# Attention stage: merged score banks, a later reciprocal, all normalising on GpSimd, q and k transposed through the projection banks, context scales a head later

## What is computed

```python
xq, wq = quant_dequant(layernorm(x)), quant_dequant(ctx)   # fp8, blocks 1x128 and 128x128
x = x + einsum('emk,enk->emn', xq, wq)
hidden = layernorm(x)                          # second layer starts here
h = rmsnorm(hidden, attn_norm_w)
q, k, v = h @ q_w.T, h @ k_w.T, h @ v_w.T      # 16 q heads, 4 kv heads of 128
q, k = rope(rmsnorm(q)), rope(rmsnorm(k))
p = softmax(causal(q k^T / sqrt(128)))
hidden = hidden + (p v) @ o_w.T
h2 = rmsnorm(hidden, ffn_norm_w)
out = x + hidden + moe(h2)                     # 8 experts, top 2, width 352
```

## Time and profile before

| | us |
|---|---|
| median of 3 runs | 1465.03 |
| lowest and highest | 1464.09, 1466.55 |
| span of the profiled execution | 1464.1 |
| PE busy over the span | 1268.7 (87%) |
| DVE, ACT, POOL busy | 838.2, 719.6, 383.0 |
| prologue | 0 to 91 |
| the 16 iterations | 91 to 1090 |
| dispatch and experts | 1100 to 1464 |

### The profile page before, as it was taken

The page is one execution under the profiler, slowest core; times in us unless marked ns, Lnnn a source line. Parts: engine busy times, 40 slices in busy tenths (PEclk is TensorE's granted clock), DMA queues, the critical chain, the costliest instruction groups (busy, mean ns, idle before and its releaser), DMA issues. The chain is left out here.

```text
span 1464.1 us, 22579 instructions
## 1 busy us (share of the span) xinstructions
PE 1268.7 (87%) x6845; PEld 1022.3 (70%) x6845; DVE 838.2 (57%) x2459; ACT 719.6 (49%) x2289; POOL 383.0 (26%) x545
## 2 busy tenths in 40 slices
PE   1867899999999989889999999989885299999995
PEld 0455676787776778677767778778664288888995
DVE  7667877666876657578757656565535022222321
ACT  6447755556675555466645655546542022222331
POOL 0223221332322223133213133223210123334332
PEclk9889999999999999999999999999997599999998
DMA  3270324350535465547535565764214786774443
GB/s 94 79 266 22 135 109 178 135 200 9 219 101 201 150 217 177 195 140 207 176 130 196 178 215 179 200 201 148 87 58 174 244 293 189 214 234 75 83 76 43
DMA packets 89444, 227.85 MB, mean 156 GB/s; under 512 B 12080, under 2 KB 49840, under 8 KB 79088
## 3 DMA queue, kind: packets, MB, share of 16 engines
q1 hardware_dynamic: 75552, 201.21, 39.2%
q0 software_dynamic: 10848, 24.71, 9.1%
q10 hardware_dynamic: 2928, 0.49, 0.2%
...
## 5 line engine op out<-in xcount | busy, mean ns | idle before, releaser
L527 POOL TENSOR_TENSOR prob<-prob,rtotal 128x128 f32<-128x128 f32 (+2 forms) x192 | 116.9, 614 | 459.1 <-DVE rtotal L1270 439.7
L1264 DVE TENSOR_SCALAR_CACHE_REDUCE prob<-bank,nscale 128x128 f32<-128x128 f32 (+3 forms) x256 | 135.0, 545 | 166.7 <-PE bank L705 166.3
L944 ACT ACTIVATE prob<-prob,bias 128x128 f32<-128x128 f32 (+3 forms) x256 | 144.8, 566 | 154.3 <-DVE prob L1264 153.5
L669 PE MATMUL bank<-w_hi,hT_hi 128*128 128x512 f32 x480 | 175.1, 365 | 15.0 <-DVE rot L1229 14.9
L724 PE MATMUL bank<-pT,v 128*128 128x512 f32 (+3 forms) x512 | 175.0, 444 | 9.7 <-ACT pT L950 9.1
L950 ACT ACTIVATE pT<-bank 128x512 f32<-128x512 f32 (+3 forms) x256 | 103.8, 433 | 140.6 <-PE bank L713 140.0
L1657 PE MATMUL gu<-we,xT_hi 128*128 x624 | 155.8, 332 | 17.0 <-SPq L1599 14.3
L669 PE MATMUL bank<-w_hi,hT_lo 128*128 128x512 f32 x480 | 163.7, 341 | 0.0
L669 PE MATMUL bank<-w_lo,hT_hi 128*128 128x512 f32 x480 | 163.6, 341 | 0.0
L504 POOL TENSOR_TENSOR r<-r,rot 128x640 f32<-128x640 f32 x60 | 99.9, 1666 | 189.8 <-DVE rot L1229 189.8
L1657 PEld LDWEIGHTS gu<-we,xT_hi 128*128 128x128 f32 x624 | 109.0, 190 | 23.4 <-issue 21.4
(11 more groups left out here) (291 smaller groups left out, 2854.5 us busy)
## 6 DMA issues: line engine op xcount, KB each, us to landing
...
```

Of the source, the lines that this page charges most:

```text
L527: nc.gpsimd.tensor_tensor(p, p, rtotal[:, 4 * h + q:4 * h + q + 1].broadcast_to([P, KEYS[q]]), ALU.mult).then_inc(prob_ready, 1)
L669: last = nc.tensor.matmul(o, hT[a][:, k, t * P:(t + 1) * P], wkv(j, c, k) if kv else wq(j, c, k), start=(k == 0 and n == 0), stop=(k == KC ...
L944: nc.scalar.activation(p, p, ACT.Exp, bias=bias[:, 4 * h + q:4 * h + q + 1], scale=-1.0, accum_out=total[:, 4 * h + q:4 * h + q + 1]).then ...
L1264: nc.vector.tensor_scalar(prob[(G * it + h) % (LAG + 1)][:, P_AT[q]:P_AT[q] + KEYS[q]], bank[SC + q % 2][:, 0:KEYS[q]], nscale[it % 2][:, ...
```

## The change

Scores go in three parts: q = 0 and 1 share one bank, q = 2 and q = 3 have one each, in turns over banks 3 and 4; q = 2 is scored before `fill(h, 1)` and q = 3 before `fill(h, 2)`. One reciprocal takes all four sums of a head, one head later, and POOL normalises all four blocks. The transposed probabilities are copied in three copies rather than four (j = 2 and 3 together). ACT takes exponentials 2 before `fill(h, 1)` and exponentials 3 before `fill(h, 2)`, but copies 0 and 1 behind `fill(h, 1)` and copy 2 behind `fill(h, 2)`. q and k are transposed in the order 1, 0, 2, 3, 4 into banks 0 and 1: 1 in `fill(3, 2)`, 0 and 2 in `fill(3, 3)`, 3 and 4 in `fill(0, 1)` of the next iteration, and the projection into these banks waits for all five. The context's maxima are taken in four parts over `fill(0, 1)` and `fill(0, 2)`, POOL's part (`ca`) stands in `fill(0, 3)`, the scales in `fill(1, 1)`. Left out below: semaphore lists, the prologue's and the tail's calls, the same functions' calls with new arguments.

```diff
@@ -98,7 +98,7 @@
-FILL = {(0, 1): (('u', 4),),
+FILL = {(0, 1): (('u', 3), ('u', 4)),
@@ -108,15 +108,16 @@
-        (3, 2): (('o', 3),),
-        (3, 3): (('t', 0), ('t', 1), ('t', 2), ('t', 3))}
-FRONT = ({(0, 1): (('cm', 0), ('cs', 0)),
-          (0, 2): (('cv', 0), ('cr', 0)),
-          (0, 3): (('cv', 1), ('cd', 0)),
-          (1, 2): (('cr', 1),),
-          (1, 3): (('cv', 2),),
+        (3, 2): (('o', 3), ('t', 1)),
+        (3, 3): (('t', 0), ('t', 2))}
+FRONT = ({(0, 1): (('cm', 0), ('cm', 1)),
+          (0, 2): (('cm', 2), ('cm', 3)),
+          (0, 3): (('ca', 0),),
+          (1, 1): (('cs', 0), ('cv', 0)),
+          (1, 2): (('cr', 0), ('cv', 1)),
+          (1, 3): (('cd', 0), ('cr', 1), ('cv', 2)),
@@ -174,6 +175,8 @@
+PARTS = ((0, 1), (2,), (3,))
+TURNS = (1, 0, 2, 3, 4)
@@ -274,7 +277,8 @@
-TR = (PT, PT + 1, AUX, PT, AUX)
+SC_AT = (0, KEYS[0], 0, 0)
+PT_COLS = (QS[0], QS[1], QS[2] + QS[3])
...
@@ -329,6 +333,19 @@
+def score_bank(s, part):
+    return bank[SC + (3 * s + part) % 2]
+def score_reads(fill):
+    return 4 * (fill // 3) + (2, 3, 4)[fill % 3] if fill >= 0 else 0
+def pt_bank(s, m):
+    return bank[PT + (3 * s + m) % 2]
+def turn_bank(i):
+    return bank[TURNS.index(i) % 2]
@@ -521,10 +538,11 @@
-    def normalise(it, h, q):
-        pool.wait_ge(inverted, 16 * it + 4 * h + q + 1)
-        p = prob[(G * it + h) % (LAG + 1)][:, P_AT[q]:P_AT[q] + KEYS[q]]
-        nc.gpsimd.tensor_tensor(p, p, rtotal[:, 4 * h + q:4 * h + q + 1].broadcast_to([P, KEYS[q]]), ALU.mult).then_inc(prob_ready, 1)
+    def normalise(s):
+        pool.wait_ge(inverted, s + 1)
+        for q in range(TT):
+            p, n = prob[s % (LAG + 1)][:, P_AT[q]:P_AT[q] + KEYS[q]], 4 * (s % G) + q
+            nc.gpsimd.tensor_tensor(p, p, rtotal[:, n:n + 1].broadcast_to([P, KEYS[q]]), ALU.mult).then_inc(prob_ready, 1)
@@ -552,27 +570,26 @@
-        work = {"kv": lambda t: add_rope(it + 1, t), "n": lambda _: newton(it + 1), "cm": lambda _: column_maxima(b + 1)}
+        work = {"kv": lambda t: add_rope(it + 1, t), "n": lambda _: newton(it + 1), "ca": lambda _: column_maxima(b + 1)}
         if g == 1 and b:
             add_hidden(b - 1)
         for h in range(G):
-            normalise(it, h, 0)
-            normalise(it, h, 1)
-            for kind, i in units(it, h, 1):
-                if kind in work:
-                    work[kind](i)
-            normalise(it, h, 2)
-            for place in (2, 3):
+            if it or h:
+                normalise(G * it + h - 1)
+            for place in (1, 2, 3):
                 for kind, i in units(it, h, place):
                     if kind in work:
                         work[kind](i)
+    normalise(G * NIT - 1)
 @block.tensor
 def _(pe):
     def transposes_x(f, t, after=None):
         n = TT * f + t
         pe.wait_ge(xd_ready, n + 1)
-        if f and t in (0, 3):
-            pe.wait_ge(qk_lo, (G + 1) * (HKV * (f - 1) + (2 if t == 0 else 3)))
+        if f and t == 0:
+            pe.wait_ge(hlo_ready, TT * f)
+            need(pe, lg_ready, TT * (f - 2))
@@ -617,7 +634,7 @@
-            pe.wait_ge(qk_lo, (G + 1) * min(HKV * (rb + 2), NIT))
+            pe.wait_ge(hlo_ready, TT * min(rb + 3, B))
@@ -661,6 +678,7 @@
+            need(pe, qk_lo, (G + 1) * j)
@@ -671,47 +689,43 @@
-        it = j - 1
-        if i == 1 and j == 0:
-            pe.wait_ge(first_added, TT)
+        turn = TURNS.index(i)
+        if turn == 0:
+            pe.wait_ge(rope_added if j else first_added, TT * (j + 1))
+            need(pe, o_added, TT * (j - 2) + 3 if j >= 2 else 0)
         if i == 0:
             pe.wait_ge(k_ready, j + 1)
-            need(pe, pt_copied, 16 * it + 4 * (G - LAG))
-        if i == 2 and j:
-            b, g = divmod(it, HKV)
-            if g == 1 and b + 1 < B:
-                pe.wait_ge(x1_ready, TT * (b + 1) + 3)
-            if g == 2 and b + 1 < B:
-                pe.wait_ge(hlo_ready, TT * (b + 2))
-            if g == HKV - 1 and b:
-                pe.wait_ge(lg_ready, TT * b)
-        if i >= 2:
-            need(pe, qk_lo, (G + 1) * j + {2: 0, 3: 1, 4: 3}[i])
+            need(pe, o_added, TT * (j - 1) if j >= 2 else 0)
+        if turn >= 2:
+            pe.wait_ge(qk_lo, (G + 1) * j + turn - 1)
         at = G * HD if i == 0 else (i - 1) * HD
         for t in range(TT):
-            last = nc.tensor.transpose(bank[TR[i]][:, t * P:(t + 1) * P], r[:, t, at:at + HD], ident[:, :])
+            last = nc.tensor.transpose(turn_bank(i)[:, t * P:(t + 1) * P], r[:, t, at:at + HD], ident[:, :])
         last.then_inc(qk_tr, 1)
-    def score(it, h, q):
-        if q == 0:
+    def score(it, h, part):
+        s = G * it + h
+        if part == 0:
             pe.wait_ge(qk_lo, (G + 1) * it + h + 2)
-        need(pe, biased, 16 * it + 4 * h + q - 1)
-        o = bank[SC + q % 2]
-        for n, (a, c) in enumerate(SPLITS):
-            nc.tensor.matmul(o[:, 0:KEYS[q]], qT[a][:, h, q * P:(q + 1) * P], kT[it % 2][c][:, 0:KEYS[q]], start=(n == 0), stop=False)
-        nc.tensor.matmul(o[:, q * P:(q + 1) * P], identb[:, :], mask[:, :], start=False, stop=True).then_inc(scored, 1)
-    def transpose_p(s, j):
-        if j == 0:
-            pe.wait_ge(prob_ready, 3 * s + 3)
-            pe.wait_ge(prob3_ready, s + 1)
-        need(pe, pt_copied, 4 * s + j - 1)
-        for q in range(j, TT):
-            last = nc.tensor.transpose(bank[PT + j % 2][:, (q - j) * P:(q - j + 1) * P],
-                                       prob[s % (LAG + 1)][:, P_AT[q] + j * P:P_AT[q] + (j + 1) * P], ident[:, :])
+        need(pe, biased, score_reads(3 * s + part - 2))
+        for q in PARTS[part]:
+            o = score_bank(s, part)[:, SC_AT[q]:SC_AT[q] + KEYS[q]]
+            for n, (a, c) in enumerate(SPLITS):
+                nc.tensor.matmul(o, qT[a][:, h, q * P:(q + 1) * P], kT[it % 2][c][:, 0:KEYS[q]], start=(n == 0), stop=False)
+            last = nc.tensor.matmul(o[:, q * P:(q + 1) * P], identb[:, :], mask[:, :], start=False, stop=True)
+        last.then_inc(scored, 1)
+    def transpose_p(s, m):
+        if m == 0:
+            pe.wait_ge(prob_ready, TT * (s + 1))
+        need(pe, pt_copied, 3 * s + m - 1)
+        at = 0
+        for j in ((0,), (1,), (2, 3))[m]:
+            for q in range(j, TT):
+                last = nc.tensor.transpose(pt_bank(s, m)[:, at:at + P], prob[s % (LAG + 1)][:, P_AT[q] + j * P:P_AT[q] + (j + 1) * P], ident[:, :])
+                at += P
@@ -720,7 +734,7 @@
-        pe.wait_ge(pt_copied, 4 * s + j + 1)
+        pe.wait_ge(pt_copied, 3 * s + min(j, 2) + 1)
...
@@ -772,9 +786,6 @@
-            if h == 0 or s == 0:
-                pe.wait_ge(qk_lo, (G + 1) * it + G)
@@ -783,19 +794,16 @@
-                values(s, 1)
-                transpose_p(s, 3)
-            score(it, h, 3)
-            if s >= 0:
-                values(s, 2)
-                values(s, 3)
+                for j in range(1, TT):
+                    values(s, j)
             fill(h, 3)
     for s in range(G * NIT - LAG, G * NIT):
-        for j in range(TT):
-            transpose_p(s, j)
-            if j:
-                values(s, j - 1)
-        values(s, TT - 1)
+        transpose_p(s, 0)
+        transpose_p(s, 1)
+        values(s, 0)
+        transpose_p(s, 2)
+        for j in range(1, TT):
+            values(s, j)
@@ -944,10 +952,10 @@
-    def copy_p(s, j):
-        act.wait_ge(pt_tr, 4 * s + j + 1)
-        need(act, pv_step, 4 * s + j - 3)
-        nc.scalar.activation(pT[:, PT_AT[j]:PT_AT[j] + QS[j]], bank[PT + j % 2][:, 0:QS[j]], ACT.Copy).then_inc(pt_copied, 1)
+    def copy_p(s, m):
+        act.wait_ge(pt_tr, 3 * s + m + 1)
+        need(act, pv_step, TT * (s - 1) + (1, 2, 4)[m] if s else 0)
+        nc.scalar.activation(pT[:, PT_AT[m]:PT_AT[m] + PT_COLS[m]], pt_bank(s, m)[:, 0:PT_COLS[m]], ACT.Copy).then_inc(pt_copied, 1)
@@ -958,9 +966,9 @@
-        act.wait_ge(qk_tr, (G + 1) * j + i + 1)
+        act.wait_ge(qk_tr, (G + 1) * j + TURNS.index(i) + 1)
         o = kT[j % 2][0][:, :] if i == 0 else qT[0][:, i - 1, :]
-        nc.scalar.activation(o, bank[TR[i]][:, :], ACT.Copy).then_inc(qk_hi, 1)
+        nc.scalar.activation(o, turn_bank(i)[:, :], ACT.Copy).then_inc(qk_hi, 1)
...
@@ -1020,22 +1028,20 @@
+            exponentials(it, h, 2)
+            fill(h, 1)
             if s >= 0:
                 copy_p(s, 0)
                 copy_p(s, 1)
-            fill(h, 1)
-            exponentials(it, h, 2)
+            exponentials(it, h, 3)
+            fill(h, 2)
             if s >= 0:
                 copy_p(s, 2)
-                copy_p(s, 3)
-            fill(h, 2)
-            exponentials(it, h, 3)
-            if s >= 0:
                 hi_attn(s)
             fill(h, 3)
     for s in range(G * NIT - LAG, G * NIT):
-        for j in range(TT):
-            copy_p(s, j)
+        for m in range(3):
+            copy_p(s, m)
...
@@ -1108,12 +1114,6 @@
-    def ctx_maxima(f):
-        for k in range(KC):
```

(48 more changed lines are left out.)

## The result

The changed kernel takes **1555.49 us** (median of 4 runs, 1552.87 to 1557.49) against 1465.1 of the kernel before on the same chip: 1.062 times as long, 95% interval 1.059 to 1.065. The forecast was 1458, with 1482 as its upper end. The profiled execution has a span of 1554.6 us.

What follows compares the result with a forecast made beforehand. PE was taken as the bound, with its idle 86.1 us and low clock to win. Terms 19 + 12 + 13 + 2 - 17 - 20 - 2 = 7 us off 1464.1, plus 0.9, gave 1458 us; range 1437 to 1482.

Steps and rivals of the forecast that it cites:

- (d): Copy 2 behind ACT's fill 2 delays values 2: loss of 20 us, bounds 5 and 30; copies 0 and 1 covered.
- R2: Rival: ACT's copy behind the fills decides, its waits and the first projection's bringing half clock: 1480 us, chance 0.28.
- R1: Rival: the waits really go, ACT and DVE being lighter than taken: 1441 us, chance 0.20.
- (a): Iteration ends, PE waiting for k's low half: 1.1 us empty at each of fifteen ends, gain of 19 us.
- (b): Low clock behind iteration ends: 17 us lost today, three short stretches left, gain of 12 us.
- (c): New wait before the next projection for the last q low half: 1.15 us in each of fifteen iterations, loss of 17.
- (e): Context scales a head later, DVE no longer standing 6.49 us for POOL's reduction: gain of 13 us, between 5 and 18.
- R3: Rival: one for one, (a) to (d) cancel and DVE's backlog eats (e): 1465 us, chance 0.12 together with R4.
- (f): DVE loses reciprocals and a pass, POOL gains a block at no cost; fewer stalls before scores: gain of 2 us.
- R4: Rival: more POOL work holds up DVE's rounding and splitting: 1461 us, chance 0.12 together with R3.

Runs made afterwards that it cites:

- exp3_behind: Changed kernel with ACT's exponentials 3 moved behind fill 2 and copy 2, copy 2 still behind fill 2: 1485.07 us (1.0121).
- score_blocks_alone: slot_order_ctx_before with q and k transposed in the old banks and slots, leaving shared score blocks, three transposed parts and POOL's late normalising: 1463.77 us (0.9982).
- qk_banks_alone: Kernel before with only the transposes of q and k in banks 0 and 1, u3 and t1 moved, ACT's order left: 1512.26 us (1.0320).
- order_by_slot: Changed kernel, ACT's exponentials 3 behind copy 2, copy 2 ahead of fill 2 except in head 3, fill 1 ahead of exponentials 2 in head 0: 1470.06 us.
- slot_order_ctx_before: order_by_slot with the context's maxima, scales and roundings in the slots of the kernel before: 1459.72 us (0.9966).

## Why the prediction was wrong, step by step

**(d), ACT's copy behind the fills, is the step that failed.** Its working counted squares (1.0), the expert piece (0.45) and the copy (0.48) behind fill 2 and left out what the change puts ahead of that fill: exponentials 3, 0.7 us themselves, which wait for a maximum that DVE makes behind its own fill 1. The term was 20 us; the wait grew by 92, 65.9 us of net idle time came with 15.5 of lost speed, and moving that one instruction gives 70 back. The prediction listed ACT's queue and did not walk DVE's.

The rest of (d) was right for copy 2 and wrong for copies 0. With exponentials 3 out of the way (exp3_behind), the wait on copy 2 is 26.4 us, 19 more than before, where the term was 20. But the wait on copies 0, which (d) took to be covered, is 22.6 against 1.8. R2, that ACT's copy decides, had the place and the sign and the same omission, so it ended at 1480. R1, that the waits really go, is out: PE's idle time rose.

**(a), the ends:** 1.1 us each forecast, 1.05 measured. That is a right number with a cause that is not shown: score_blocks_alone has ends as short with the old banks (9.1 us on `kT_lo`, 0.7 on `hT_lo`), and qk_banks_alone, which has the new banks, waits 32.6 us on `kT_lo`.

**(b), the clock behind ends:** half clock rises from 66.4 to 107.8 us in the change. The sign held once ACT's order was mended: 57.2 in exp3_behind, 56.3 in order_by_slot and 42.7 in slot_order_ctx_before. In the last PE was busy in 36.9 us of it against 50.5 before, a gain of 7 in speed where 12 were forecast.

The rule quoted from the Trainium skill, TensorE: Matmul & The Clock Gate, section "A second HAM failure mode: psum-queue depth-cycling", would have the many short waits swing the clock. In iterations 12 to 14 of the change, with fifteen waits of up to 1.2 us (9 for copies, 3 for `kT_lo`, 3 for `qT_lo`, 13.0 us in all), the clock stayed full; this row speaks against it here:

```profile
954.00:1129.30 175.30, 162.18 (x900) 127.63 (x900) 92.88 (x261) 92.79 (x317) 65.30 (x97) 1.00 0.52 167
```

**(c), the wait for u4:** 1.15 us each forecast, 1.0 measured, 15 times. **(e), the context:** the wait on `rot` went as forecast and came back before the scores. DVE's wait on POOL's maxima went as forecast too (three waits of at most 0.7 us in the change, where 6.49 was one of them before), but the part's price was 8 us instead of a gain of 13. The R3 clause that DVE's backlog eats it was nearer. **(f):** 2 us of gain forecast, 4 measured.

**R4:** the collision exists: DVE's second rounding pass took 1.67 us beside Pool. Its mean rose from 737 to 913 ns over 24 passes, 4 us of DVE in all (the kernel before, then the changed one); it is no cause of 90. And R4 had the wrong instruction. Of the ten such passes of the change that took over 0.9 us, eight lie beside Pool's 640-column addition of the rotated parts (L521, L504 before), which the kernel before has too: there six rounding passes took 1.64 to 1.68 us beside it and nine of L1275 1.31 to 1.59. Only two, of 1.14 us, lie beside a normalising.

```profile
L1100 DVE TENSOR_SCALAR xm<-xm 128x512 f32<-128x512 f32 x24 | 17.7, 737 | 0.8
```
```profile
L1106 DVE TENSOR_SCALAR xm<-xm 128x512 f32<-128x512 f32 x24 | 21.9, 913 | 0.8
```

The forecast also put 0.9 us between span and time; in the change's profiled run it is 1.8 (1554.6 and 1556.43), which changes nothing.

What stays open: what shortens the ends of iterations; why order_by_slot still stands 10 us above slot_order_ctx_before when PE's waits on DVE are alike; and whether Pool's fourth block costs DVE anything that reaches PE, which one pair of runs could not resolve.
